# Folding the input through all head matrices first, in four column strips, and weighing all heads into one bank

## The chip, the cores and the metric

The kernel runs on one core of a Trainium2 chip. The metric is the device time of one execution in microseconds (us), from the first to the last instruction. Three runs of the kernel before gave 2040.4, 2041.68 and 2044.19 us; the median is 2041.68 us. The core's engines run side by side and meet through semaphores: PE (TensorE, matrix products, results in the eight PSUM banks), PEld (its weight loads), DVE (VectorE), ACT (ScalarE), POOL (GpSimd) and SP (the queue that starts DMAs). Each engine works off its own instructions in the order in which they are written.

## The reference, cut to what matters

The input is x, 2 x 1024 tokens of 128 features. It is normalised, and the output is x plus two branches of the normalised input: one latent attention layer over the full causal length, and a stack of six layers of windowed attention and gated feed-forward. The change touches the stack:

```python
for i in range(DEPTH):                       # 6 layers
    x = attn_layer(shift_tokens(x), Wqkv[i], q_scale[i], k_scale[i], Wo[i]) + x
    x = ffn_layer(shift_tokens(x), ln_g[i], ln_b[i], W1[i], b1[i], W2[i], b2[i]) + x

def attn_layer(x, Wqkv, qs, ksc, Wo):        # 16 heads of 64, window 32
    q, k, v = split_heads(x @ Wqkv)
    q = rotary(l2norm(q) * qs) ; k = rotary(l2norm(k) * ksc)
    attn = softmax(8 * q @ k_own_and_previous_block, masked)
    return concat_heads(attn @ v) @ Wo

def ffn_layer(x, g, bln, W1, b1, W2, b2):
    a, gate = split((layernorm(x) * g + bln) @ W1 + b1)   # 2 x 341
    return a * gelu(gate) @ W2 + b2
```

shift_tokens takes the upper 64 features from the token before. For one head the output is P (x Wv) Wo, where P is 32 queries by 64 keys for each block of 32 tokens. Both kernels form the folded matrices M_h = Wv_h Wo_h, 128 x 128, once a layer (16 heads), and so need no values or head outputs of their own.

## The kernel before, in words

The stack works on 96 tiles of 128 tokens (16 tiles a layer, 6 layers), in a software pipeline. Each engine has one list of stages, written out by hand in a loop `for G in range(STEPS)`; in step G a stage works on tile G, G-1, G-2 and so on, whatever its argument says. Nothing but these lists and the waits on semaphores sets the order of the work.

For a tile PE projects keys and queries (`project`, float32r in three products of an upper and a lower part, six matmuls of 512 columns each), transposes keys and queries by head pairs (`transposes`, eight of 128x128), writes a mask into banks 4 and 5 and adds the scores onto it (`mask_scores`, `scores`, 64 small matmuls), transposes the softmax's result (`transpose_probs`), and then applies it. Banks 0 and 1 hold a projection, 2 and 3 transposes, 4 and 5 the scores, 6 and 7 everything small and the feed-forward. A stage that writes a bank first claims it: `claim` waits until the last reader of the bank is done (the dictionary `freed`).

The application of the probabilities is what the change replaces. Before, `input_rows` transposes the shifted input back into rows (L1324), ACT copies it (L710), SP copies it by ten DMAs a tile into windows of 64 rows (L351 to L354, doubled on two halves of the partitions), `weigh` multiplies rows of the input by the probabilities, 64 keys deep (two halves of four matmuls of 256 columns, banks 4 and 5), ACT copies the result (L717, L723), and `fold` multiplies it by the sixteen M_h (16 matmuls of 128x128 with 128 columns, bank 7). The sum lies with features on the partitions. DVE adds it to X (`attended`, L981); two transposes and a copy bring rows for the layer norm (`ln_rows`, L1399).

On DVE a step has for keys and for queries a cosine product (L934), a sine product (L939) and a sum of squares (L961, L966), then denominators, moments, maxima and subtraction of the softmax, and `seeds` (L992, L994, L997, L1000), four small operations on 33 columns, which begin a reciprocal square root. ACT goes on with it in `roots` (a logarithm and an exponential, L764, L766) and POOL ends it in `refine` (L501). POOL also adds cosine and sine products (L471, L476), scales keys, queries and probabilities (L507, L513, L466). Every four tiles make a chunk of 512 tokens for the feed-forward: `up_gate`, `up_value` (3 matmuls each, three slices j = 0, 1, 2 of 341), the gelus on ACT (L774) and `down`. The gelu needs another table of functions on ACT than logarithm and exponential; after gelu j = 2 the line `act.preload_act_table_set("natural_log_exp_and_others")` (L777) fetches the latter, and the compiler puts a load in front of any other activation whose function the table in force lacks.

## Time and profile before

| quantity | value |
|---|---|
| median of 3 runs | 2041.68 us (2040.4 to 2044.19) |
| the profiled execution, its own time | 2045.28 us |
| its span, first to last instruction | 2043.4 us |
| busy: PE, DVE, ACT, POOL | 1873.4, 1656.8, 1264.6, 1331.1 us |
| granted PE clock, mean | 0.982 |
| ACT table loads in the program | 50 |

The span has three stretches. To about 365 us the latent attention runs, which the change leaves as it is but for where a few arrays lie. From 368.6 to 1966.4 us the 96 tiles enter the pipeline one after the other, and the rest is the pipeline running empty. Busy time is time in which at least one instruction of an engine runs; PE's matmuls overlap, so that the length of a piece of PE's work is best read from the start of it to the start of the next.

### The profile page before, as it was taken

The page shows a single profiled execution, that of the slowest core. Times are in us where ns is not written, and L with a number is a line of the kernel's source. Part 1 is how long each engine was busy: PE and PEld are TensorE (multiplying, and loading weights), DVE is VectorE, ACT ScalarE, POOL GpSimd, SP SyncE. Part 2 cuts the span into 40 slices and gives each one's busy share as a digit, 9 for nine tenths or more (in the row PEclk, how much of TensorE's full clock was granted, in tenths as well). Part 3 has the DMA queues.
Part 4 walks back from the last instruction along what each step waited for, and adds up shares of the span by engine and source line. Part 5 has one row for each costly group of instructions (what it writes and reads, how often), then busy time and mean ns, then how long its engine had stood idle before and what let it go on. Part 6 is the DMA issues. An engine that isn't in the chain of part 4 may idle for free.

```text
span 2043.4 us, 61163 instructions
## 1 busy us (share of the span) xinstructions
PE 1873.4 (92%) x24364; PEld 1471.0 (72%) x24364; DVE 1656.8 (81%) x2684; ACT 1264.6 (62%) x2082; POOL 1331.1 (65%) x1146
## 2 busy tenths in 40 slices
PE   6888887598999999999999999999999999999996
PEld 4655656477777777777777777777777777777774
DVE  4866866577888898898879998898989889887873
ACT  5766665355666566656655666566666666665653
POOL 3322334477778776787767886777777778776760
PEclk9999998799999999999999999999999999999999
DMA  3000000011001110010111101100111001000001
GB/s 106 2 0 0 0 1 6 22 38 38 22 18 24 39 40 17 22 25 18 39 38 22 24 19 39 37 22 22 25 39 38 20 21 24 18 18 15 19 18 27
DMA packets 76933, 50.06 MB, mean 24 GB/s; under 512 B 17216, under 2 KB 74240, under 8 KB 75008
## 3 DMA queue, kind: packets, MB, share of 16 engines
q1 hardware_dynamic: 76672, 46.39, 9.0%
q8 instruction: 187, 3.06, 0.6%
q14 instruction: 74, 0.61, 0.1%
HBM read 20.11 MB, written 1.05 MB: 10 GB/s over the span
## 4 chain that ended last, share of the span: by engine, by line
PE 62%; DVE 23%; issue 9%; ACT 4%; POOL 1%; DMA 1%; DVEq 0%; SPq 0%; ACTq 0%; POOLq 0%
PE banks L1101 44%; PE banks L1258 9%; DVE arena L939 4%; PE banks L1310 4%; DVE arena L934 3%; DVE small L885 2%; PE banks L1185 2%; DVE small L1005 2%; DVE small L966 2%; PE banks L1299 1%; DVE lnx L1020 1%; DVE small L961 1%; DVE arena L1048 1%; DVE small L997 1%; DVE small L972 1%
## 5 line engine op out<-in xcount | busy, mean ns | idle before, releaser
L1101 PE MATMUL banks<-arena 128*128 128x128 f32 (+3 forms) x4516 | 450.9, 280 | 32.3 <-DMA arena<-in_wqT_dram 10.1
L1101 PEld LDWEIGHTS banks<-arena 128*128 128x128 f32 (+3 forms) x4516 | 426.5, 173 | 69.8 <-issue 19.1
L471 POOL TENSOR_TENSOR arena<-arena 128x1024 f32<-128x1024 f32 x96 | 228.8, 2383 | 110.0 <-DVE arena L939 110.0
L934 DVE TENSOR_TENSOR arena<-banks,tabs 128x1024 f32<-128x1024 f32 x192 | 234.3, 1220 | 62.4 <-PE banks L1258 52.7
L703 ACT ACTIVATE arena<-banks 128x1024 f32<-128x1024 f32 x96 | 98.6, 1027 | 230.9 <-PE banks L1258 230.9
L939 DVE TENSOR_TENSOR arena<-banks,tabs 128x1024 f32<-128x1024 f32 x192 | 232.9, 1213 | 0.2 <-issue 0.2
L466 POOL TENSOR_TENSOR prob<-prob,small 128x1024 f32<-128x1024 f32 x96 | 182.8, 1904 | 74.2 <-DVE small L974 70.3
L476 POOL TENSOR_TENSOR arena<-arena 128x1024 f32<-128x1024 f32 x96 | 228.5, 2380 | 0.0
L1101 PE MATMUL banks<-arena,xwr 64*128 64x256 f32 x1536 | 217.8, 402 | 11.3 <-ACT arena L717 11.3
L1101 PE MATMUL banks<-qkH,xsH 128*128 128x512 f32 x384 | 173.7, 452 | 39.6 <-DVE arena L939 39.6
L1258 PE MATMUL banks<-cst,arena 128*128 128x128 f32 x1536 | 209.5, 280 | 0.1
L513 POOL TENSOR_TENSOR arena<-arena,small 128x1024 f32<-128x1024 f32 x96 | 185.1, 1928 | 14.0 <-POOL arena L476 0.4
L1258 PEld LDWEIGHTS banks<-cst,arena 128*128 128x128 f32 x1536 | 176.7, 143 | 21.0 <-issue 1.7
L1101 PEld LDWEIGHTS banks<-arena,xwr 64*128 64x128 f32 x1536 | 132.2, 186 | 81.7 <-issue 47.8
L501 POOL TENSOR_TENSOR small<-small 128x33 f32<-128x33 f32 x100 | 24.7, 247 | 248.3 <-ACT small L766 248.3
L507 POOL TENSOR_TENSOR arena<-arena,small 128x1024 f32<-128x1024 f32 x96 | 182.8, 1904 | 4.4
L966 DVE TENSOR_REDUCE small<-arena 128x16 f32<-128x1024 f32 x96 | 116.8, 1216 | 83.3 <-ACT arena L679 82.9
L394 POOL TENSOR_TENSOR gqs<-arena,cst 128x128 fp32r<-128x128 f32 x112 | 46.0, 411 | 186.9 <-PE banks L1101 157.2
L668 ACT ACTIVATE arena<-banks 128x1024 f32<-128x1024 f32 x96 | 98.5, 1026 | 95.5 <-PE banks L1101 95.5
L1101 PE MATMUL banks<-qkH,xsL 128*128 128x512 f32 x384 | 155.1, 404 | 0.0
L1101 PE MATMUL banks<-qkL,xsH 128*128 128x512 f32 x384 | 154.2, 402 | 0.0
L1310 PE MATMUL banks<-arena 64*32 64x64 f32 x12288 | 143.8, 226 | 10.4 <-issue 9.1
(135 smaller groups left out, 4217.6 us busy)
## 6 DMA issues: line engine op xcount, KB each, us to landing
xwr<-xwr SPq DMA_DIRECT2D x576, 32.0 KB, 1.9
qkraw<-in_wqk_dram SPq DMA_DIRECT2D x6, 1024.0 KB, 5.2
arena<-in_wvo_dram SPq DMA_DIRECT2D x6, 1024.0 KB, 5.2
xwr<-xwr SPq DMA_DIRECT2D x384, 16.0 KB, 1.8
W<-in_w_dram SPq DMA_DIRECT2D x6, 341.0 KB, 3.1
W<-in_w_dram SPq DMA_DIRECT2D x6, 192.0 KB, 2.7
res<-in_x_dram SPq DMA_DIRECT2D x4, 256.0 KB, 4.2
tabc<-in_tab_dram SPq DMA_DIRECT2D x1, 1024.0 KB, 7.5
```

The lines of the kernel that those rows point to most:

```text
L466: pool.tensor_tensor(p, p, over(den[:, :], 64), ALU.mult).then_inc(s["p_nrm"], 1)
L471: pool.tensor_tensor(kc, kc, ks, ALU.add).then_inc(s["k_add"], 1)
L476: pool.tensor_tensor(qc, qc, qs, ALU.add).then_inc(s["q_add"], 1)
L507: pool.tensor_tensor(heads(kc), heads(kc), over(rs[:, 4, 0:LH], LD), ALU.mult).then_inc(s["k_nrm"], 1)
L513: pool.tensor_tensor(heads(qc), heads(qc), over(rs[:, 4, LH:2 * LH], LD), ALU.mult).then_inc(s["q_nrm"], 1)
L703: act.activation(ptile[:, :, :], two(2).rearrange("p (k t) -> p k t", k=NP), ACT.Copy).then_inc(s["pt_cp"], 1)
L934: dve.tensor_tensor(heads(c), heads(two(0)), table(k % NT, kind), ALU.mult).then_inc(s[done], 1)
L939: dve.tensor_tensor(w.rearrange("p (h z k) -> p h z k", h=LH, z=2), swapped(two(0)), table2(k % NT, kind + 1), ALU.mult).then_inc(s[done], 1)
L966: dve.reduce_sum(rin[:, LH:2 * LH], heads(sqq), AXX).then_inc(s["q_ss"], 1)
L1101: return pe.matmul(o, l, r, start=start, stop=stop)
L1258: ins = pe.transpose(bk(2 + k // 4)[:, P * (k % 4):P * (k % 4 + 1)], src[:, P * k:P * (k + 1)], ident)
L1310: ins = pe.matmul(bk(4 + o)[WIN * w:WIN * (w + 1), 64 * j:64 * (j + 1)], qT[r, j, WIN * w:WIN * (w + 1)], kT[r, j, WIN * w:WIN * w + 64], ...
```

## The change

Products are taken in the other order. The shifted input, 32 tokens at a time (stationary, 128x32), is multiplied by all sixteen M_h at once: `values`, two groups a tile, eight matmuls of 512 columns each, four of them side by side in the four 32-column strips of the array, each with another quarter of M as its moving operand. ACT copies each group of 64 tokens (two banks, 1024 columns) into a ring of six (`vw`). Then `weigh` multiplies by the transposed probabilities, 128 keys-by-heads deep, again in four strips (one for each block of 32 queries), 32 matmuls of 128 columns into one bank, which is the weighed sum of all heads, with tokens on the partitions. Gone are `input_rows`, the row copy, the ten DMAs a tile, `fold` and the two copies between `weigh` and `fold`. The probabilities lie otherwise for this (own half and previous half apart), so that the access patterns of `subtract`, `denominators` and `scale_probs` change, not their sizes.

Since the sum now has tokens on the partitions, the residual stream (`Xt`) is kept so too. `ln_rows` becomes a product with a shifted unit matrix, a second one of 32 rows takes the token before the tile, and ACT copies 64 columns twice. `down` swaps its operands (12 matmuls of 128 columns for 3 of 512, the same number of columns, b2 as a row of W2). Once a chunk PE transposes the new stream into columns (`layer_columns`, four transposes) and ACT copies it (`copy_layer`).

`seeds` moves from DVE to POOL, right in front of `refine`. `normalise_rows` is a scalar_tensor_tensor in place of a tensor_scalar. And the lists of stages of all engines are written in a new order with other lags; STEPS grows from 107 to 108. On SP the loads of the next layer's weights no longer stand behind the row DMAs and their waits. `lower_shifted` on POOL is one operation of 128x512 for two of 64x512 and a memset. The diff, cut:

```diff
-STEPS = DEPTH * TILES + 11
+STEPS = DEPTH * TILES + 12
-M_BANK, XT_BANK, DN_BANK = 7, 6, 7
+PV_BANK, V_BANK, XT_BANK, DN_BANK, LN_BANK = 6, 4, 7, 7, 7
...
+            def values(k, g):
+                b, i = tile_at(k)
+                pe.wait_ge(s["xs"], 2 * (k // 4) + 2)
+                pe.wait_ge(s["M_H"], 2 * (k // TILES) + 2)
+                claim(V_BANK, V_BANK + 1)
+                for z in range(2):
+                    t0 = P * i + 64 * g + WIN * z
+                    for q in range(NQ):
+                        ins = pe.matmul(bk(V_BANK + z)[WIN * q:WIN * (q + 1), :], xs[:, b, t0:t0 + WIN],
+                                        M[:, q, :, :].rearrange("p m n -> p (m n)"), start=True, stop=True, skip_group_check=True)
...
+            def weigh(k):
...
+                    for z in range(2):
+                        for m in range(NQ):
+                            for w in range(NW):
+                                ins = pe.matmul(bk(PV_BANK)[WIN * w:WIN * (w + 1), 0:D], ptile[:, NQ * z + m, WIN * w:WIN * (w + 1)],
+                                                block_of(k, w - 1 + z)[:, D * m:D * (m + 1)],
+                                                start=(z, m) == (0, 0), stop=(z, m) == (1, NQ - 1), skip_group_check=True)
...
+            def copy_values(k, g):
+                act.wait_ge(s[f"v_mm{g}"], k + 1)
+                after(act, "o_mm", k - 2 + g)
+                act.activation(vw[:, (2 * k + g) % RV, :], two(V_BANK), ACT.Copy).then_inc(s[f"v_cp{g}"], 1)
...
# DVE: normalise_rows
-                    dve.tensor_scalar(lnx[:, :], lns[:, k % 2, :], ag[:, k % 2, 0:1], rs[:, 4, 32:33], ALU.subtract, ALU.mult)\
+                    dve.scalar_tensor_tensor(lnx[:, :], lns[:, k % 2, :], ag[:, k % 2, 0:1],
+                                             rs[:, 4, 32:33].to_broadcast([P, D]), ALU.subtract, ALU.mult).then_inc(s["ln_x"], 1)
...
# POOL, list of stages (new)
+                next_table(G - 2)
+                lower_columns(G - 7)
+                rotate_keys(G - 1)
+                scale_probs(G - 3)
+                shifted_lower(chunk_at(G, 15))
+                seeds(G - 1)
+                refine(G - 1)
+                scale_keys(G - 1)
+                next_query_weights(G - 1)
+                rotate_queries(G - 1)
                 lookback(G - 1)
...
# ACT, list of stages (new)
+                copy_columns(G - 6)
+                copy_values_upper(G - 2)
+                roots(G - 1)
+                gelu(chunk_at(G, 10), 0)
+                copy_layer(chunk_at(G, 14))
...
+                copy_probs(G - 3)
+                gelu(chunk_at(G, 11), 1)
...
+                gelu(chunk_at(G, 10), 2)
                 square_keys(G)
+                shifted_upper(chunk_at(G, 14))
+                copy_rows(G - 4)
+                exponentials(G - 2)
+                copy_keys(G - 1)
+                copy_values_lower(G - 1)
                 square_queries(G)
# DVE, list of stages (new)
+                maxima(G - 2)
                 normalise_rows(G - 5)
+                gated(chunk_at(G, 11), 0)
+                subtract(G - 2)
                 cosine_keys(G)
                 sine_keys(G)
+                attended(G - 3)
+                denominators(G - 2)
+                moments(G - 4)
                 sum_keys(G)
+                sum_queries(G)
+                cosine_queries(G)
+                gated(chunk_at(G, 11), 1)
+                sine_queries(G)
+                gated(chunk_at(G, 11), 2)
+                residual(chunk_at(G, 12))
```

PE's list shows best in the built programs. Before, in the step in which the gate slice j = 2 (85 columns wide) is computed, PE has behind the transposes of the queries:

```order
L1101 MATMUL banks<-xnH,W1H 85x512
L1101 MATMUL banks<-xnH,W1L 85x512
L1101 MATMUL banks<-xnL,W1H 85x512
L1101 MATMUL banks<-arena 128x128 x8
L1407 MATMUL banks<-cst,lnx 128x128
L1299 MATMUL banks<-bfc 128x512 x2
L1101 MATMUL banks<-arena 128x128 x8
L1310 MATMUL banks<-arena 32x64 x64
L1258 MATMUL banks<-cst,prob 128x128 x8
```

The other two gate slices stand earlier in that same step, behind the transposes of the keys, and the scores are followed by the transposes of the probabilities. Now, in the step that computes the gate slices 0 and 2 (L1311 is `values`, L1438 `layer_columns`, L1286 the mask, L1245 the transposes, L1297 the scores):

```order
L1311 MATMUL banks<-M,xs 32x512 x8
L1089 MATMUL banks<-xnw,w1w 128x512 x3
L1438 MATMUL banks<-cst,Xt 128x128 x4
L1286 MATMUL banks<-bfc 128x512 x2
L1245 MATMUL banks<-cst,prob 128x128 x8
L1297 MATMUL banks<-arena 32x64 x64
L1089 MATMUL banks<-xnw,w1w 85x512 x3
```

Gate slice 2, which uses bank 6 as slice 0 does, now stands right behind the scores and in front of the projection of the keys (six rows at L1089 that follow).

On ACT, the step with the gelus before (L774 gelu, L764 and L766 `roots`, L679 and L697 copies for the queries):

```order
L774 ACT_TABLE_LOAD
L774 ACTIVATE arena<-banks,b1p 128x512
L723 ACTIVATE arena<-banks 128x2x512
L774 ACTIVATE arena<-banks,b1p 128x512
L679 ACTIVATE arena<-banks 128x1024
L774 ACTIVATE arena<-banks,b1p 85x512
L777 ACT_TABLE_LOAD
L697 ACTIVATE arena<-banks 128x1024
L756 ACTIVATE xnf<-banks 128x128
L757 ACTIVATE xnH<-banks 128x128
L764 ACTIVATE small<-small 128x33
L766 ACTIVATE small<-small 128x33
```

All three gelus share one load in front and one behind, and `roots` has none. The same place now (L719 `copy_values_upper`, L773 and L775 `roots`, L783 gelu, L592 and L593 `copy_layer`, L714 `copy_probs`, L786 the preload, L679 the squares of the keys):

```order
L719 ACTIVATE arena<-banks 128x1024
L773 ACT_TABLE_LOAD
L773 ACTIVATE small<-small 128x33
L775 ACT_TABLE_LOAD
L775 ACTIVATE small<-small 128x33
L783 ACT_TABLE_LOAD
L783 ACTIVATE arena<-banks,b1p 128x512
L592 ACTIVATE xs<-banks 64x512
L593 ACTIVATE xs<-banks 64x512
L714 ACTIVATE arena<-banks 128x1024
L783 ACTIVATE arena<-banks,b1p 85x512
L786 ACT_TABLE_LOAD
```

The gelu of slice 1 has moved to the step after the preload; `roots` has a load in front of the logarithm and another in front of the exponential. The whole program has 230 table loads where it had 50: 67 each at L773 and L775, 48 at L783, 24 at L786, 22 in front of the softmax's exponential (L745), 2 at the start.

## Rows read from the trace of the kernel before

**Rows 1.** The page: busy time, share of the span and instructions by engine.
```profile
PE 1873.4 (92%) x24364; PEld 1471.0 (72%) x24364; DVE 1656.8 (81%) x2684; ACT 1264.6 (62%) x2082; POOL 1331.1 (65%) x1146
```

**Rows 2.** Stretches: length, busy PE, PEld, DVE, ACT, POOL (instructions), clock, DMA share, GB/s.
```profile
700.00:1900.00 1200.00, 1158.45 (x16133) 918.01 (x16131) 1050.41 (x1425) 765.95 (x1136) 893.91 (x660) 1.00 0.11 27
...
1966.00:2043.40 77.40, 59.74 (x605) 42.81 (x603) 37.98 (x75) 35.23 (x59) 21.07 (x21) 0.98 0.10 25
```

**Rows 3.** The squares of the keys: ns min/median/max, first and last start.
```profile
L668 ACT ACTIVATE arena<-banks x96: 1024/1026/1032, 368.6 to 1966.4; 128x1024 f32<-128x1024 f32 x96
```

**Rows 4.** Waits from 700 to 1900 us: total, times, longest us.
```profile
POOL small L501 <- ACT small L766: 169.7, 71, 4.9
...
PE banks L1101 <- DVE arena L939: 20.7, 30, 0.9
```

**Rows 5.** PE in order of time, one step: start, us, instruction, shapes, count.
```profile
1203.53 0.28 PE L1324 MATMUL banks<-cst,X 64*128 64x64 f32 x2
1203.74 1.09 PE L1258 MATMUL banks<-cst,arena 128*128 128x128 f32 x8
...
1207.41 1.13 PE L1101 MATMUL banks<-arena,xwr 64*128 64x256 f32 x8
1208.48 0.50 PE L1101 MATMUL banks<-qkH,xsH 128*128 128x512 f32 x1
...
1209.97 1.03 PE L1258 MATMUL banks<-cst,arena 128*128 128x128 f32 x8
1210.84 1.95 PE L1101 MATMUL banks<-arena 128*128 128x128 f32 x16
1212.63 0.27 PE L1407 MATMUL banks<-cst,lnx 128*128 128x128 f32 x1
1212.73 0.59 PE L1299 MATMUL banks<-bfc 128*128 128x512 bf16 x2
1213.17 1.95 PE L1101 MATMUL banks<-arena 128*128 128x128 f32 x16
1215.04 1.48 PE L1310 MATMUL banks<-arena 64*32 64x64 f32 x128
1216.46 1.09 PE L1258 MATMUL banks<-cst,prob 128*128 128x128 f32 x8
```

**Rows 6.** PE in the latent attention, matmuls in four 32-column strips, and what follows.
```profile
310.75 1.74 PE L1101 MATMUL banks<-arena 128*32 128x128 f32 x56
312.42 0.44 PE L1185 MATMUL banks<-cst,arena 128*128 128x128 f32 x2
```

**Rows 7.** ACT in order of time: the softmax's exponential, a table load, a gelu.
```profile
1258.09 1.05 ACT L741 ACTIVATE prob<-prob 128x1024 f32<-128x1024 f32 x1
1259.15 1.28 ACT L774 ACT_TABLE_LOAD   x1
1260.44 0.69 ACT L774 ACTIVATE arena<-banks,b1p 128x512 f32<-128x512 f32 x1
```

**Rows 8.** In order of time: `seeds`' last operation, `roots` on ACT, `refine` on POOL.
```profile
1215.14 1.25 DVE L1000 TENSOR_TENSOR small<-small 128x33 f32<-128x33 f32 x1
...
1216.42 0.23 ACT L764 ACTIVATE small<-small 128x33 f32<-128x33 f32 x1 [3.04 <-DVE small L1000]
...
1216.69 0.23 ACT L766 ACTIVATE small<-small 128x33 f32<-128x33 f32 x1
1217.06 0.25 POOL L501 TENSOR_TENSOR small<-small 128x33 f32<-128x33 f32 x1 [0.71 <-ACT small L766]
```

**Rows 9.** Groups from 700 to 1900 us: busy us, mean ns, idle before.
```profile
L513 POOL TENSOR_TENSOR arena<-arena,small 128x1024 f32<-128x1024 f32 x70 | 135.5, 1936 | 10.0
...
L412 POOL TENSOR_TENSOR xsL<-X,xsH 64x512 fp32r<-64x512 f32 x18 | 23.4, 1300 | 1.4
...
L939 DVE TENSOR_TENSOR arena<-banks,tabs 128x1024 f32<-128x1024 f32 x141 | 170.9, 1212 | 0.0
L1020 DVE TENSOR_SCALAR lnx<-lns,small 128x128 f32<-128x128 f32 x70 | 91.4, 1306 | 0.0
```

More of the change, by code:

```diff
@@ L22 @@
 AXX = mybir.AxisListType.X
+AXXY = mybir.AxisListType.XY
 P = 128
@@ L244, in chunk_at, with columns @@
             return c if (G - lag) % 4 == 0 and 0 <= c < DEPTH * NC else None
+        def columns(c):
+            b, t0 = divmod(c % NC * CH, T)
+            return X[:, b, t0:t0 + CH]
         def layer_at(G, lag):
@@ L746, in copy_rows, with copy_layer @@
                     after(act, "ln_x", k - 1)
-                    act.activation(lns[:, k % 2, :].rearrange("p (z c) -> p z c", z=2),
-                                   two(6).rearrange("p (z c) -> p z c", z=2)[:, :, 0:64], ACT.Copy).then_inc(s["ln_cp"], 1)
+                    act.activation(lns[:, k % 2, 64:D], bk(LN_BANK)[:, 0:64], ACT.Copy).then_inc(s["ln_cp"], 1)
+                    act.activation(lns[:, k % 2, 0:64], Xt[:, k % TILES, 0:64], ACT.Copy).then_inc(s["ln_cp"], 1)
+            def copy_layer(c):
+                if c is not None and c < (DEPTH - 1) * NC:
+                    act.wait_ge(s["xT_mm"], c + 1)
+                    shifted(c + NC, bk(XT_BANK))
             def copy_columns(k):
@@ L1313, in scores @@
                     ins.then_inc(s["s_mm"], 1)
-            def input_rows(k):
-                if is_tile(k):
-                    b, i = tile_at(k)
-                    after(pe, "x_new", k // 4 - NC + 1)
-                    claim(XT_BANK, XT_BANK + 1)
-                    for z in range(2):
-                        r = slice(64 * z, 64 * z + 64)
-                        c0 = XO + P * i - z
-                        ins = pe.transpose(bk(XT_BANK + z)[:, XT_COL:XT_COL + 64], X[r, b, c0:c0 + P], ident[r, 64 * z:64 * z + 64])
-                    ins.then_inc(s["xT_mm"], 1)
-                    freed[XT_BANK] = freed[XT_BANK + 1] = ("xT_cp", k + 1)
@@ L1328, in weigh @@
-            def weigh(k, half):
-                claim(4, 5)
-                for w2 in range(2):
-                    w = 2 * half + w2
-                    for o in range(2):
-                        r = slice(64 * o, 64 * o + 64)
-                        ins = mm(bk(4 + o)[:, 256 * w2:256 * (w2 + 1)].rearrange("p (k t) -> p k t", k=NP),
-                                 xw[r, k % 2, w, :], ptile[r, :, WIN * w:WIN * (w + 1)])
-                ins.then_inc(s["z_mm"], 1)
-                freed[4] = freed[5] = ("z_cp", 2 * k + half + 1)
@@ L1341, in weigh_lower, with values_lower, values_upper @@
+            def values_lower(k):
+                if is_tile(k):
+                    values(k, 0)
+            def values_upper(k):
+                if is_tile(k):
+                    values(k, 1)
+            def weigh(k):
                 if is_tile(k):
                     pe.wait_ge(s["pt_cp"], k + 1)
[L1343 to L1356 removed]
+                    pe.wait_ge(s["v_cp0"], k + 1)
+                    pe.wait_ge(s["v_cp1"], k + 1)
+                    pe.wait_ge(s["vw_0"], 1)
+                    claim(PV_BANK)
+                    for z in range(2):
[4 more added lines that the diff above has]
+                                                start=(z, m) == (0, 0), stop=(z, m) == (1, NQ - 1), skip_group_check=True)
+                    ins.then_inc(s["o_mm"], 1)
+                    freed[PV_BANK] = ("x1", k + 1)
@@ L1392, in ln_rows @@
                 if is_tile(k):
-                    b, i = tile_at(k)
+                    n = k % TILES
                     pe.wait_ge(s["x1"], k + 1)
-                    claim(6, 7)
-                    for z in range(2):
-                        r = slice(64 * z, 64 * z + 64)
-                        c0 = 1 + P * i - z
-                        ins = pe.transpose(bk(6 + z)[:, 0:64], X1[r, b, c0:c0 + P], ident[r, 64 * z:64 * z + 64])
+                    claim(LN_BANK)
+                    ins = mm(bk(LN_BANK)[:, 0:64], next_row, Xt[:, n, 64:D])
+                    if n % NT:
+                        ins = pe.matmul(bk(LN_BANK)[0:32, 0:64], first_row, Xt[96:P, n - 1, 64:D], start=False, stop=True,
+                                        skip_group_check=True)
                     ins.then_inc(s["lnT_mm"], 1)
-                    freed[6] = freed[7] = ("ln_cp", k + 1)
+                    freed[LN_BANK] = ("ln_cp", 2 * k + 2)
             def ln_columns(k):
```

402 lines of the change are left out of this document (157 added, 245 removed).

## The prediction

> **What bounds the kernel now.** I began with busy time by engine: PE is busy for 92% of the span [rows 1]. The table of stretches then says where: from 700 to 1900 us PE is busy for 1158.45 of 1200 us at a full clock, DVE for 1050, POOL for 894, ACT for 766 [rows 2]. The squares of the keys mark one step a tile; 95 steps lie between 368.6 and 1966.4 us, so a step takes 16.82 us [rows 3], and 1200 us hold 71.3 of them. Per step PE is busy 16.24 us and idle 0.58, DVE busy 14.7, POOL 12.5, ACT 10.7. The list of waits shows what idles PE: the sine product on DVE for 20.7 us in 30 waits, so 0.29 us a step [rows 4]. POOL has slack, and shows it as a wait of 2.4 us a step for ACT's roots, 169.7 us in all [rows 4]. So PE's own work sets the pace, with DVE 2 us behind it. A change is worth what it takes from PE's step, if no loop through ACT, DVE and POOL becomes longer than PE's step.
>
> **PE's work.** I read lengths from start to start [rows 5]. Removed per tile: input rows 1203.53 to 1203.74, 0.2 us; two halves of weighing at 1207.41 to 1208.48, 2 x 1.07 = 2.14; two halves of folding, 1.79 + 1.87 = 3.66. Sum 6.0 us. Added: the trace has the new shape in the latent attention. There 8 key blocks in 4 strips make 64 records of 128 columns (each float32 matmul leaves two; 56 of the 64 are in the trace), and they take 310.75 to 312.42 = 1.67 us [rows 6]. `weigh` now is 64 such records, 1.67 us; a group of `values` is 16 records of 512 columns, as many columns, again 1.67 us. Three times that is 5.0; for leaving and entering the strips I add 0.3, so 5.3 us. The row product for the layer norm has full weights and a second part of 32 rows: +0.2. `layer_columns` is four transposes a chunk, 4 x 0.11 over 4 steps: +0.1. `down` keeps its columns; its 24 records at 1.79/16 = 0.11 us give 2.7 us a chunk, as now. PE's unstalled step is 16.24 - 6.0 + 5.3 + 0.3 = 15.85 us. The unknown in it is a strip matmul of 512 columns. From below, 1.67 us a group is already four strips at once. From above, the scores are the nearest row that packs less well: 128 records of 64 columns in eight tiles take 1.42 us [rows 5], so 1024 columns per tile, against 2048 per tile in 1.67 us; at the scores' pace the three groups would take 3 x 2.84 = 8.5 us. I take 1.67, whose shape is the same.
>
> Here a page speaks against the change. The Trainium skill, "TensorE: Matmul & The Clock Gate", Part 3, on measured speedup, gives four packed tiles 3.07 times and three column strips 2.38 times the rate of one, not four and three. By that rule 5.0 us become 5.0 x 4 / 3.07 = 6.5, 1.5 us more a step. The 1.67 us of rows 6 disagree with it.
>
> **DVE.** It loses the four seeds, of which the last alone took 1.25 us for 33 columns in rows 8, while POOL's 0.25 us for as many columns is the least that one can cost. So at least 1 us a step goes. `normalise_rows` takes 1.31 us on average for 128 columns [rows 9], of which the columns explain little. The new form costs between 0.25 us, the price of a small operation, and 1.3 as now; I take 1.0, near its own row. DVE falls below 13.7 us a step, no bound by sum.
>
> **POOL.** It loses one of two operations of 1.3 us a chunk (-0.35 us a step [rows 9]) and gains four seeds. The nearest price of a small operation there is `refine`, 0.25 us [rows 8]; with a handoff between dependent ones 4 x 0.32 = 1.3. So 13.5 us busy, 13.8 with gaps. But `seeds` and `refine` now stand next to each other, and POOL sits idle while ACT does the roots. At best that is what the trace shows, 1216.39 (end of the seed) to 1217.06 = 0.67 us [rows 8].
>
> **ACT, and the term that decides.** Copies come out even (two of 1.03 us for two). But the built program has 230 table loads for 50, 10 in 4 steps where there were 2. A load takes 1.28 us, and the gelu follows 0.01 us behind its end [rows 7]. That is +2.6 us a step, ACT at 13.6 us: again no bound by sum, but ACT's list is in order and other engines wait in it. The Trainium skill, "ScalarE: Activation LUTs", What ACT_TABLE_LOAD costs, adds a drain of about 1.38 us to the 1.283 us of a load. Rows 7 show none: exponential ends 1259.14, load starts 1259.15. With a drain the chain of three loads below would be 3 x 1.38 = 4.1 us longer in one step of four.
>
> Let t be the end of the second group of `values` on PE. ACT copies it: t+1.15. In three steps of four a load for the logarithm (to t+2.45), the logarithm, a load (to t+4.0) and the exponential follow: roots end at t+4.2. In the step of gate slices 0 and 2 comes a third load and the gelu of slice 0: t+5.5, t+6.25. PE meanwhile does gate slice 0 (0.75), layer_columns (0.45), mask (0.44), transposes (0.87 and a switch, 1.05) and scores (1.42) [rows 5], so that at t+4.15 it stands before gate slice 2, whose bank 6 is freed by that gelu. First loss: 6.35 - 4.15 = **2.2 us**. ACT goes on: two column copies (to 7.5), probabilities (8.5), gelu 2 (9.2), the preload (10.5), and only then the squares of the keys (11.55). DVE's cosine and sine products (2 x 1.21) follow to t+14.0, and PE's next projection, the queries, needs their end: 14.1. PE itself would be there at 6.35 + 0.7 (gate) + 1.5 (keys) + 0.95 (transposes) + 0.5 (rows) + 1.75 + 1.75 (weigh, values) = 13.5. Second loss: **0.6 us**.
>
> In the step with up-value slices 1 and 2 the path is POOL's. From the start P of the queries' projection, t = P+4.3. DVE needs after sine_keys 0.3 + 1.4 + 0.6 + 1.15 + 1.15 us to the sum of the queries, so seeds end at P+5.9 = t+1.6, before the logarithm's load is over. Roots end t+4.2, refine t+4.6, scaled keys +1.94 [rows 9] = t+6.6. PE wants them for its transposes at t + 1.5 + 0.44 + 1.05 + 1.42 + 1.5 = t+5.9. Loss **0.7 us**. In the step with `down` that is covered by its 2.7 us. In the step without loads in `roots`, gated slice 0 (0.74 us) stands in front of the subtraction on DVE: from the scores' end maxima 1.35, normalise 1.0, gated 0.74, subtract 1.15, cosine 1.15, sine 1.21 and handoffs 0.3 are 6.9 us, against PE's 6.4 (keys 1.5, transposes 0.9, rows 0.5, weigh 1.75, values 1.75). Loss **0.5 us**.
>
> Together 2.2 + 0.6 + 0.7 + 0.5 = 4.0 us in 4 steps, 1.0 a step. The step is 15.85 + 1.0 = 16.85, and for the loops that pass within 0.3 us of PE's (POOL's ring in a step with loads is 13.8 + 2.9 = 16.7) I add 0.05: **16.9 us**.
>
> **Edges.** Four more column copies on ACT as the latent attention starts, 4 x 0.6 = 2.4 us at most. The pipeline runs empty in 77.4 us over 11 steps [rows 2]; a twelfth is added and the last transposes go. I take +5 us for both, between 0 and 12. The row DMAs go, ten a tile; they cost nothing now, since no DMA is among the waits of PE in rows 4's stretch, and the weights' loads on SP, which stood behind them, can only come earlier. The latent stretch, 365 us, stays.
>
> **Sum.** 95 x (16.90 - 16.82) = +8, +5: 13 us more than the profiled execution's 2045.28, so 2058. That execution stood 3.6 us above the median, against which the forecast is 2041.7 + 13 = 2055, say **2054 us**. What PE saves (0.4 us a step of work and most of 0.58 us idle) goes back into table loads.
>
> **Rivals.**
> A. The loads are hidden better. For it: ACT is busy 13.6 of 16.9 us, and if seeds come late the logarithm's load is over before them; against it: the gelu chain has three loads in a row whatever seeds do. If only 1.8 us in four steps are lost, the step is 16.3, and the time 2041.7 - 49 + 5 = **1997 us**; with nothing lost 15.95 a step, 1964.
> B. POOL's ring becomes the bound. It decides from where the round trip over ACT is longer than 16.9 - 13.8 = 3.1 us, that is, when seeds end more than 0.2 us after ACT was ready and both loads lie open behind each other's waits, or when the small operations cost 0.5 us each in place of 0.3. At 17.5 us a step: 2041.7 + 65 + 5 = **2111 us**, slower. For it: rotation, three scalings and seeds leave POOL no room; against it: one step in four has no loads and lets it catch up.
> C. Four strips don't run at four times the pace. Rows 6 speak against it, though only for 128 columns. At 2.2 us a group, between rows 6 and the scores' pace, it is +1.6 us a step and **2204 us**. By the 3.07 of the Trainium skill's "TensorE: Matmul & The Clock Gate" it would be 1.5 x 95 more than the forecast, 2197 us.
> D. A load holds ACT for longer than its row when another load or an exponential comes right behind. Rows 7 show 0.01 us behind a load; if the chain were 4 us longer in one step of four, it would be +95 us, **2149 us**. It is the drain of the Trainium skill's "ScalarE: Activation LUTs".
>
> **How the numbers follow.** Forecast 0.47, A 0.32, B 0.16, C 0.03, D 0.02. A difference of 0.2%, 4 us, is about what a measurement of this kernel can tell. The forecast's own range is 2030 to 2080: of its 0.47, 0.07 is faster than 2037.6, 0.10 is within 0.2%, 0.30 slower. A is faster for 0.30 and the same for 0.02; B, C and D are slower. Faster 0.37, same 0.12, slower 0.51. The range runs from inside A (below 1985 I leave 0.08) to B's middle (above 2112, 0.11).
>
> **What would show it.** In the profile after: `weigh` and each `values` group near 1.7 us from start to start (right: PE's work per step 15.8 to 16); table loads busy about 295 us in all; in one step of four an idle PE in front of gate slice 2, released by a gelu; POOL's `refine` waiting for ACT 2 to 3 us a step; the transposes of the keys waiting for POOL. Wrong: no gap before gate slice 2 (then A), POOL above 90% busy or waiting nowhere else than for the roots (B), strips above 2 us a group (C).

## The result, and the profile after

The changed kernel takes **2081.29 us** (median of 4 runs, 2079.05 to 2089.52), the kernel before beside it 2041.04 us (4 runs, 2037.65 to 2044.19). The ratio is 1.0205, 95% interval 1.0172 to 1.0238: slower by 40 us. The forecast was 2054 us, slower by 13; the measured time lies 1 us above the forecast's own range (2030 to 2080) and well inside the outer one (1985 to 2112).

The profiled execution spans 2080.7 us. Its busy row, to be held against [rows 1]:

```profile
PE 1849.6 (89%) x29444; PEld 1308.2 (63%) x29444; DVE 1529.7 (74%) x2286; ACT 1501.6 (72%) x2286; POOL 1399.4 (67%) x1494
```

PE works 24 us less than before, and ACT 237 us more. Next the stretch of [rows 2] (length, then busy PE, PEld, DVE, ACT, POOL, clock, DMA share, GB/s), and the squares of the keys, which mark a step as in [rows 3]:

```profile
700.00:1900.00 1200.00, 1110.02 (x19216) 775.74 (x19219) 925.57 (x1110) 922.17 (x1253) 916.68 (x879) 0.99 0.03 10
```
```profile
L679 ACT ACTIVATE arena<-banks x96: 1005/1025/1032, 363.5 to 1996.0; 128x1024 f32<-128x1024 f32 x96
```

A step is (1996.0 - 363.5) / 95 = 17.18 us, where it was 16.82. Of the 37 us between the two spans the 95 steps make 1632.5 - 1597.8 = 35, the start is 5 us earlier and the drain (1996.0 to 2080.7 us, before 1966.4 to 2043.4) some 8 us longer. The 1200 us hold 69.8 steps. In each of them PE is busy for 15.90 us, where it was 16.24, and idle for 1.29, where it was 0.58. So PE's work did shrink, and its idle time grew by twice as much. The waits in that stretch say what ended the idle time (engine, tile and line, released by; total us, times, longest):

```profile
POOL small L506 <- ACT small L775: 154.2, 68, 3.3
...
DVE arena L943 <- ACT arena L679: 64.1, 21, 3.6
...
PE banks L1089 <- ACT arena L783: 38.6, 17, 2.3
...
PE banks L1297 <- issue: 16.3, 24, 1.0
...
PE banks L1089 <- DVE arena L948: 10.4, 33, 0.3
PE banks L1335 <- DVE arena L1039: 10.2, 15, 1.3
...
PE banks L1245 <- ACT M L731: 8.2, 4, 2.2
...
PE banks L1311 <- DVE prob L1001: 2.3, 5, 0.6
...
PE banks L1245 <- POOL arena L512: 0.6, 1, 0.6
```

Read the rows that begin with PE. The largest is the wait of gate slice 2 (L1089) for a gelu (L783), 17 times 2.3 us, once in four steps; in [rows 4] the largest was the sine product, 20.7 us in 30 waits. The sine product (L948) is now 10.4. New are the scores' "issue" (L1297: nothing that the profile shows was waited for), the weighing's wait (L1335) for the gated product (L1039), and, at a change of layer, the transposes (L1245) behind ACT's copy of the next folded matrices (L731).

The table loads on ACT, by the line of the operation that they stand in front of (count in the stretch, busy us, mean ns, idle before):

```profile
L773 ACT ACT_TABLE_LOAD x51 | 65.4, 1283 | 0.9
L775 ACT ACT_TABLE_LOAD x51 | 65.4, 1283 | 0.9
L783 ACT ACT_TABLE_LOAD x34 | 43.6, 1283 | 0.6
...
```

L773 and L775 are logarithm and exponential of `roots`, L783 the gelus. The preload (L786) and the softmax's exponential (L745) have 17 more each: 170 loads, 218 us. Here is one step of the gate, cut to the rows that follow one another (start, us, engine and line, in brackets the idle time before and its releaser):

```profile
1199.17 1.92 PE L1311 MATMUL banks<-M,xs 128*32 128x512 f32 x16
...
1201.02 0.96 PE L1089 MATMUL banks<-xnw,w1w 128*128 128x512 f32 x3
...
1201.16 1.03 ACT L719 ACTIVATE arena<-banks 128x1024 f32<-128x1024 f32 x1 [0.52 <-PE banks L1311]
...
1202.21 1.28 ACT L773 ACT_TABLE_LOAD   x1
...
1203.66 1.49 PE L1297 MATMUL banks<-arena 64*32 64x64 f32 x128
1203.75 1.28 ACT L775 ACT_TABLE_LOAD   x1
1205.05 0.23 ACT L775 ACTIVATE small<-small 128x33 f32<-128x33 f32 x1
...
1205.29 1.28 ACT L783 ACT_TABLE_LOAD   x1
...
1206.59 0.69 ACT L783 ACTIVATE arena<-banks,b1p 128x512 f32<-128x512 f32 x1
...
1207.42 0.90 PE L1089 MATMUL banks<-xnw,w1w 128*85 128x512 f32 x3 [2.27 <-ACT arena L783]
...
1210.01 1.28 ACT L786 ACT_TABLE_LOAD   x1
...
1211.30 1.02 ACT L679 ACTIVATE arena<-banks 128x1024 f32<-128x1024 f32 x1
...
1212.42 1.23 DVE L943 TENSOR_TENSOR arena<-banks,tabs 128x1024 f32<-128x1024 f32 x1 [3.56 <-ACT arena L679]
...
1214.92 0.47 PE L1089 MATMUL banks<-qkH,xsH 128*128 128x512 f32 x1 [0.29 <-DVE arena L948]
```

The values' second group starts at 1199.17 and PE goes on at 1201.02, the prediction's t. ACT copies it, loads for the logarithm, loads for the exponential, loads for the gelu, and the gelu of slice 0 ends at 1207.28, t+6.26, where t+6.25 was worked out. PE had finished the scores and stood idle for 2.27 us. Then gelu 2 and the preload hold up the squares of the keys (L679); DVE waits 3.56 us for them, and its sine product releases the queries' projection at 1214.92, 0.29 us late.

### The profile page after: what moved, and what is told of

Its sections match the earlier page's. It is cut to its first block and busy times, and to the rows that moved or that the text cites. A ratio compares the mean times of both kernels' runs of the same rounds, so it can differ in the third digit from the quotient of the medians.

```text
span 2080.7 us, 70693 instructions
## 1 busy us (share of the span) xinstructions
PE 1849.6 (89%) x29444; PEld 1308.2 (63%) x29444; DVE 1529.7 (74%) x2286; ACT 1501.6 (72%) x2286; POOL 1399.4 (67%) x1494
## 5 line engine op out<-in xcount | busy, mean ns | idle before, releaser
L1311 PE MATMUL banks<-M,xs 128*32 128x512 f32 x3072 | 369.0, 596 | 3.8 <-DVE prob L1001 3.6
L995 DVE TENSOR_REDUCE small<-banks 128x16 f32<-128x1024 f32 x96 | 117.5, 1224 | 211.2 <-PE banks L1297 211.2
L719 ACT ACTIVATE arena<-banks 128x1024 f32<-128x1024 f32 x192 | 197.2, 1027 | 100.2 <-PE banks L1311 97.3
L948 DVE TENSOR_TENSOR arena<-banks,tabs 128x1024 f32<-128x1024 f32 x192 | 232.7, 1212 | 0.0
L1245 PE MATMUL banks<-cst,arena 128*128 128x128 f32 x1536 | 204.9, 277 | 2.4 <-POOL arena L512 1.7
L1335 PE MATMUL banks<-arena 128*32 128x128 f32 x6144 | 190.4, 276 | 11.0 <-DVE arena L1039 10.6
L1245 PEld LDWEIGHTS banks<-cst,arena 128*128 128x128 f32 x1536 | 179.2, 142 | 29.2 <-issue 5.0
L1089 PE MATMUL banks<-qkH,xsH 128*128 128x512 f32 x384 | 172.5, 449 | 23.6 <-DVE arena L948 21.8
L1089 PE MATMUL banks<-xnw,w1w 128*128 128x512 f32 (+1 forms) x432 | 130.1, 430 | 57.0 <-ACT arena L783 55.8
L1335 PEld LDWEIGHTS banks<-arena 128*32 128x32 f32 x6144 | 164.7, 111 | 20.9 <-issue 14.2
L1311 PEld LDWEIGHTS banks<-M,xs 128*32 128x32 f32 x3072 | 90.2, 109 | 137.4 <-issue 135.0
L679 ACT ACTIVATE arena<-banks 128x1024 f32<-128x1024 f32 x96 | 98.3, 1024 | 105.8 <-PE banks L1089 105.5
L1297 PE MATMUL banks<-arena 64*32 64x64 f32 x12288 | 150.7, 227 | 22.5 <-issue 22.5
L1297 PEld LDWEIGHTS banks<-arena 64*32 64x32 f32 x12288 | 130.0, 106 | 44.0 <-issue 44.0
```

Of the source, the lines that this page charges most:

```text
L719: act.activation(vw[:, (2 * k + g) % RV, :], two(V_BANK), ACT.Copy).then_inc(s[f"v_cp{g}"], 1)
L948: dve.tensor_tensor(w.rearrange("p (h z k) -> p h z k", h=LH, z=2), swapped(two(0)), table2(k % NT, kind + 1), ALU.mult).then_inc(s[done], 1)
L1089: return pe.matmul(o, l, r, start=start, stop=stop)
L1245: ins = pe.transpose(bk(2 + k // 4)[:, P * (k % 4):P * (k % 4 + 1)], src[:, P * k:P * (k + 1)], ident)
L1297: ins = pe.matmul(bk(4 + o)[WIN * w:WIN * (w + 1), 64 * j:64 * (j + 1)], qT[r, j, WIN * w:WIN * (w + 1)], kT[r, j, WIN * w:WIN * w + 64], ...
L1311: ins = pe.matmul(bk(V_BANK + z)[WIN * q:WIN * (q + 1), :], xs[:, b, t0:t0 + WIN], M[:, q, :, :].rearrange("p m n -> p (m n)"), start=True ...
```

## The experiments

All times are medians, and ratios are to the kernel before, run beside them (2046.76 us in the first set: e1 to e4; 2045.48 in the second: e5, e6, e7, e9; 2048.4 in the third: e10, e11).

**e1, no loads in `roots`.** One more preload, behind gelu 1; the built program has 98 table loads, not 230.

```diff
-                    if j == LAST_GELU:
+                    if j in (1, LAST_GELU):
                         act.preload_act_table_set("natural_log_exp_and_others")
```

> The changed kernel with one more preload of the set that holds logarithm and exponential, behind the gelu of slice 1: 98 table loads in the program for 230, none left in roots. Theory L (the loads are what ate the saving): the wait before gate slice 2 (2.27 us in each of 24 steps, 55.8 us in the whole trace) goes, POOL's wait for the roots falls from 2.3 to about 0.7 us a step, and the step falls from 17.18 us to 16.1-16.4: 1985 to 2010 us. Rival P (PE's own work in strips, with the gaps in the scores, is what made it slower, and the loads lie beside it): not more than 15 us come back, 2065 to 2081 us.

Measured: 2002.84 us, ratio 0.9795 (0.9754 to 0.9837). A step is 16.35 us. Its stretch and three of its waits:

```profile
700.00:1900.00 1200.00, 1157.04 (x20371) 813.24 (x20370) 960.96 (x1167) 837.45 (x1216) 966.94 (x928) 1.00 0.03 10
```
```profile
POOL small L506 <- ACT small L775: 44.1, 73, 0.6
...
PE banks L1297 <- issue: 21.7, 26, 1.2
PE banks L1335 <- DVE arena L1039: 11.3, 14, 1.3
...
PE banks L1089 <- ACT arena L783: 0.2, 1, 0.2
```

The wait before gate slice 2 falls from 38.6 to 0.2 us, POOL's for the roots from 154.2 to 44.1, and the wait for the folded matrices is gone from the list. One line in ACT's program turns the change from 2% slower into 2% faster. That is the loads' price where they stand: 78 us by the medians, 84 by the ratios, 0.83 us a step by the trace. Of the 0.83, PE's idle time makes 0.70 (1.29 to 0.59 a step) and its busy time 0.13 (15.90 to 15.77), although PE's work is the same; the section on the prediction comes back to this.

**e4, the loads put into the kernel before.** The converse: without the preload the compiler places 91 + 91 + 26 = 208 loads there, for 50.

```diff
-                    if j == LAST_GELU:
-                        act.preload_act_table_set("natural_log_exp_and_others")
```

> The kernel before without its preload behind the gelus: the compiler then puts 91 loads each before logarithm and exponential of roots, 208 loads for 50. Theory L: the round trip over ACT grows by 1.3 to 2.6 us in three of four steps. POOL waited 2.4 us a step there, but scaled keys are needed at once by PE, and DVE's list goes on behind: 40 to 110 us slower, 2080 to 2150 us. Rival P: ACT is busy 10.7 of 16.8 us in that kernel, the loads fall into its idle time: within 15 us of 2041.

Measured: 2049.94 us, ratio 1.0021 (0.9996 to 1.0047): no difference that can be told. The loads are there, ACT's busy time in the stretch rises from 765.95 [rows 2] to 924.48 us, and POOL's wait for the roots from 169.7 [rows 4] to 266.0:

```profile
700.00:1900.00 1200.00, 1158.20 (x16131) 915.91 (x16129) 1025.01 (x1419) 924.48 (x1261) 891.04 (x660) 1.00 0.11 26
```
```profile
POOL small L501 <- ACT small L766: 266.0, 71, 7.6
```

PE is busy for 1158.20 us of it, as before. The expectation that loads cost by their number fell. In the order of before the one who waits behind them is POOL, and it has the slack for it.

**e10, fewer loads in one place only.** In the step in front of a gate step the logarithm's set is fetched early, behind the softmax's exponential.

```diff
                 exponentials(G - 2)
+                if chunk_at(G + 1, 10) is not None:
+                    act.preload_act_table_set("natural_log_exp_and_others")
```

> The changed kernel with the set of logarithm and exponential fetched once a chunk right behind the softmax's exponential of the step before gate slices 0 and 2, so that roots has no loads in that step and in the two around it that had none or lose them, while one step in four (with up-value slices 1 and 2) keeps both: 162 loads for 230. Theory L (the chain of three loads in front of the gelu of slice 0 carries most of the loss, as the predicted 2.8 of 4.0 us in four steps): the wait before gate slice 2 goes, and of the 78 us that the second preload won at least two thirds come, 2005 to 2030 us. Rival E (the loads cost by their number, spread over all steps): of 132 loads that the second preload saved 68 go, so half of 78 us, 2035 to 2050 us.

Measured: 2025.58 us, ratio 0.9894 (0.9857 to 0.9932). The expectation miscounted the loads: the built program has 210, since two steps of four keep both loads of `roots`. So it is even clearer than was planned: 20 loads fewer than the changed kernel's 230, and 3.1% or 63 us come back by the ratios, where e1 took 132 away for 4.1% or 84. The wait before gate slice 2 (here L1091) is down to nothing:

```profile
PE banks L1091 <- ACT arena L783: 0.5, 2, 0.3
```

e1, e4 and e10 together show that a load costs by the chain that it stands in.

**e2, the gelu ahead of `roots`.** The gate no longer waits behind the two other loads; the program has 254.

```diff
-                roots(G - 1)
                 gelu(chunk_at(G, 10), 0)
+                roots(G - 1)
```

> The changed kernel with the gelu of slice 0 written ahead of roots on ACT, loads left as the compiler puts them (254 for 230). Theory L: the wait before gate slice 2 goes (2.27 us in one of four steps, 54 us in all), but roots end later (behind a gelu and its load, 2 us) so that POOL's scaled keys come later in that step, and the squares of the keys stay late: 10 to 30 us faster than the changed kernel, 2050 to 2070 us. Rival P: the wait is PE's slack in another place, within 5 us of 2081.

Measured: 2113.9 us, ratio 1.0339 (1.0295 to 1.0383), so 1.3% slower than the changed kernel, against the expectation. The wait of the gate for the gelu is gone, and in its place stands this:

```profile
PE banks L1245 <- POOL arena L512: 38.7, 18, 2.3
```

The roots come later, POOL scales the keys later, and PE's transposes of the keys (L1245) wait the same 2.3 us. The chain of three loads has two customers, and the order only chooses which of them is late. That alone would be an even exchange, 38.7 us for 38.6. The step is 17.54 us for 17.18 because PE also idles 0.16 us more a step in smaller waits and because its busy time, for the same work, grows by 0.19: its clock is lower more often (see below).

**e7, the waiting instruction moved.** Gate slice 2 goes behind the transposes of the keys on PE.

```diff
-                up_gate(chunk_at(G, 10), 2)
                 next_shifts(chunk_at(G, 12))
                 project_keys(G)
                 transpose_keys(G - 1)
+                up_gate(chunk_at(G, 10), 2)
```

> The changed kernel with gate slice 2 behind the transposes of the keys in PE's list, loads as they are. It takes away the wait of 2.27 us in front of gate slice 2, but not ACT's chain: the copy of the probabilities, on which those transposes wait, and the squares of the keys stay behind the loads, and gelu 2 comes later. Theory L (ACT's chain, not the bank): the wait turns up again in front of the transposes of the keys and the queries' projection, within 15 us of 2081. Rival W (the wait before gate slice 2 is the loss itself): 30 to 54 us faster, 2027 to 2050 us.

Measured: 2145.28 us, ratio 1.0498 (1.0463 to 1.0534), 2.9% or some 60 us slower than the changed kernel. Both expectations were wrong. Waits, and a piece of ACT in order of time:

```profile
DVE arena L943 <- ACT arena L679: 108.2, 20, 7.2
...
PE banks L1245 <- ACT arena L714: 48.0, 17, 2.8
ACT arena L783 <- PE banks L1089: 46.2, 16, 3.5
```
```profile
1245.49 0.68 ACT L783 ACTIVATE arena<-banks,b1p 85x512 f32<-85x512 f32 x1 [3.43 <-PE banks L1089]
...
1247.49 1.02 ACT L679 ACTIVATE arena<-banks 128x1024 f32<-128x1024 f32 x1
```

PE reaches the gate without waiting, but later; now gelu 2 waits 3.43 us for it on ACT, and the preload and the squares of the keys behind it come later still. DVE's wait for them grows from 64.1 to 108.2 us. I had moved the waiter and lengthened the chain. A step is 17.86 us, 0.68 more: 0.45 of it is idle time of PE and 0.22 busy time for the same work, at a lower clock.

**e3, the old form of `normalise_rows`.** Only the form goes back; the two read the same numbers.

```diff
-                    dve.scalar_tensor_tensor(lnx[:, :], lns[:, k % 2, :], ag[:, k % 2, 0:1],
-                                             rs[:, 4, 32:33].to_broadcast([P, D]), ALU.subtract, ALU.mult).then_inc(s["ln_x"], 1)
+                    dve.tensor_scalar(lnx[:, :], lns[:, k % 2, :], ag[:, k % 2, 0:1], rs[:, 4, 32:33], ALU.subtract, ALU.mult)\
+                       .then_inc(s["ln_x"], 1)
```

> The changed kernel with the tensor_scalar of the kernel before in normalise_rows. The new form takes 1546 ns on average for 128 columns where the old took 1306. Theory L: DVE waits for PE's scores 2.1 us a step, so the form costs nothing but in steps where the subtraction is late: within 5 us of 2081. Rival N (the new form waits more for POOL and delays subtraction and sine products): the mean falls back to 1.3 us and the time by 10 to 20 us.

Measured: 2084.39 us, ratio 1.0185 (1.0143 to 1.0228), the changed kernel's within the intervals. The group in the changed kernel (700 to 1900 us), and in e3 (whole span):

```profile
L1010 DVE SCALAR_TENSOR_TENSOR lnx<-lns,small 128x128 f32<-128x128 f32 x69 | 106.7, 1546 | 0.0
```
```profile
L1010 DVE TENSOR_SCALAR lnx<-lns,small 128x128 f32<-128x128 f32 x96 | 146.7, 1528 | 8.2 <-POOL small L506 8.2
```

1546 and 1528 ns: the form changes nothing. I had put the new form at 1.0 us.

**e5 and e6, `seeds` back on DVE,** behind the sum of the queries; e5 from the changed kernel, e6 from e1. The four operations are the same.

```diff
                 shifted_lower(chunk_at(G, 15))
-                seeds(G - 1)
                 refine(G - 1)
...
                 sum_queries(G)
+                seeds(G)
                 cosine_queries(G)
```

> The changed kernel with seeds back on DVE, behind sum_queries, loads as they are. Theory L (ACT's chain of loads and gelu sets the step; POOL's list only matters through it): seeds end at about the same time on either engine, so within 8 us of 2081. Rival R (with seeds in front of refine, POOL's own ring of 13.8 us and the round trip is what the loads lengthen): POOL gets 1.1 us a step back, 20 to 50 us faster, 2030 to 2060 us.

> The kernel with the second preload (2003 us) and seeds on DVE as well. POOL waits there 1.8 us a step for the sine product, DVE 2.1 us for the scores, so neither is bound by its sum. Theory: within 6 us of 2003, so that the move of seeds to POOL earns nothing here. Rival R: POOL's relief shows, 10 to 20 us faster. Rival D (the seeds' small operations wait on DVE for POOL, as 1.25 us did for one of them in the kernel before, and make the sine product of the queries late): 8 to 25 us slower.

Measured: e5 2072.16 us, ratio 1.0148 (1.0114 to 1.0183); e6 1986.49 us, ratio 0.9724 (0.9691 to 0.9756), the fastest kernel here. e6 lies 16 us under e1 and e5 some 12 (0.6% by the ratios) under the changed kernel; the intervals of e6 and e1 just touch, and those of e5 and the changed kernel overlap by little. e6's step is 16.23 us for e1's 16.35. Its stretch and waits:

```profile
700.00:1900.00 1200.00, 1167.96 (x20506) 821.04 (x20505) 1044.46 (x1473) 842.78 (x1230) 900.74 (x644) 1.00 0.03 10
```
```profile
DVE small L994 <- PE banks L1297: 73.9, 65, 2.0
PE banks L1297 <- issue: 18.1, 24, 1.2
...
PE banks L1335 <- DVE arena L1038: 4.5, 7, 0.7
```

DVE works 84 us more than in e1 and yet less waits for it: the weighing's wait for the gated product falls from 11.3 to 4.5 us, and PE is busy for 97.3% of the stretch. DVE stood idle anyway, 153.3 us for the scores in e1 and now 73.9.

**e9, one strip of four.** From e1; three quarters of the folded matrices are left out of the attention, so that a group of `values` has 4 records of 512 columns and not 16.

```diff
-                    for q in range(NQ):
+                    for q in range(1):
```

> The kernel with the second preload, in which values computes the first of the four strips alone and copies 32 partitions of it (three quarters of the folded matrices are left out of the attention; the ring is zeroed once). Theory S (the four strips run side by side): a group keeps the length of one strip's columns, 4 records of 512 columns at about 0.43 us = 1.7 us of the 1.9 now, and the time falls by at most 2 x 0.25 us a step, 1980 to 2003 us. Rival C (the strips share the columns' rate in part, as a packing of 3.07 would have it): a group falls to 1.3 us or less and the time to 1900 to 1960 us.

Measured: 1988.89 us, ratio 0.9733 (0.9702 to 0.9764). A group and what follows it on PE, in e9 and then in e1:

```profile
1209.07 1.88 PE L1312 MATMUL banks<-M,xs 128*32 128x512 f32 x4
1210.88 0.50 PE L1090 MATMUL banks<-qkH,xsH 128*128 128x512 f32 x1
```
```profile
1213.35 1.92 PE L1311 MATMUL banks<-M,xs 128*32 128x512 f32 x16
1215.20 0.49 PE L1089 MATMUL banks<-W,arena 128*128 128x128 f32 x2
```

From start to start 1.81 us with one strip and 1.85 with four: the other three ride along for 0.04 us. e9 is 0.6% faster than e1 all the same, though the two intervals overlap a little; PE's part of that is 2 x 0.04 x 95 = 8 us. The smaller copies on ACT and the scores' gaps (10.6 us in 14 for 21.7 in 26) may make the rest, which I did not separate.

**e11, the scores ahead of the transposes of the probabilities,** from e6.

```diff
-                transpose_probs(G - 3)
                 scores(G - 2)
+                transpose_probs(G - 3)
```

> The kernel with the second preload and seeds on DVE (1986 us), with PE's scores in front of the transposes of the probabilities. PE's work is the same. DVE waits there 1.0 us a step for the scores and would get them 0.9 us earlier, which PE can only use if it waits for DVE; it waits 0.1 us a step for it. Theory (PE's own work is the bound, busy 97.3%): 1978 to 1990 us. Rival (the loop from the maxima to the projection of the queries still sets the step): 10 to 20 us faster, 1966 to 1978 us; and if copies of the transposed queries are late for the scores, slower by up to 20 us.

Measured: 2007.51 us, ratio 0.9803 (0.9765 to 0.9842), slower than e6 by 16 us by the ratios and 21 by the medians. PE idles for 52.6 us of the stretch, where it was 32.0. The largest of its waits is new:

```profile
PE banks L1089 <- ACT arena L764: 14.7, 18, 0.9
```

L764 is the gelu in this kernel. In the trace the one that waits, 18 times and mostly 0.93 us, is the first product of `ln_rows`: it uses bank 7, which the gelu of slice 1 reads. The wait of the queries' projection for the sine product grows from 5.8 to 13.6 us beside it. There was nothing left to win by this exchange.

## Why the prediction was right in sign and short in size

The mechanism was the one that the prediction named: PE saves work and gives it back to table loads that stand in the ordered list of ACT. The forecast was a step of 16.90 us; it is 17.18. Of this come 0.28 x 95 = 27 us; the edges cost 3 us for the 5 forecast, and so the profiled spans stand 37 us apart and not 13 (the medians 40). By the prediction's own steps:

**PE's work, 15.85 us a step: 15.90 measured,** and 15.77 in e1. Inside it, a group of strips was put at 1.67 us with 0.3 for all switches; start to start it is 1.85 us (1199.17 to 1201.02). So the added strips cost some 0.25 us more than worked out, and something else at least as much less than worked out; which part, no row here settles.

**PE's clock: a term that the sum did not have.** The prediction worked at a full clock. Behind some of its waits PE works on for a while at a granted clock of 0.50, which is 1.2 GHz in place of 2.4. Here is one wait before gate slice 2; the first row is a stretch of 1 us, whose granted clock of 0.50 stands third from its end:

```profile
715.00:716.00 1.00, 0.84 (x2) 0.62 (x3) 1.00 (x2) 0.97 (x3) 1.00 (x2) 0.50 0.00 0
```
```profile
715.16 1.55 PE L1089 MATMUL banks<-xnw,w1w 128*85 128x512 f32 x3 [2.28 <-ACT arena L783]
716.50 0.63 PE L1089 MATMUL banks<-qkH,xsH 128*128 128x512 f32 x1
```

The same two rows at the full clock take 0.90 and 0.40 us (1207.42 and 1208.16). From 700 to 1900 us the clock falls so 9 times in the changed kernel: 4 times behind a wait for the gelu (of 17 such waits), twice behind the folded matrices' copy and 3 times behind a gap in the scores; the kernel before and e1 have 3 falls each. Why only some of the waits are followed by one is not shown. Taken over slices of 1 us, what the clock lacks of 1.00 adds up to 15.4 us here, 5.1 before, 5.1 in e1, 25.6 in e2 and 33.9 in e7. As an estimate, this is the time lost while PE is busy: 0.22 us a step for 0.07 before, so 0.15 of the 0.36 by which the step grew, or some 14 of the 40 us. Two things agree with it: PE's busy time falls by 0.13 us a step in e1, whose work is the same, and the mean clock was 0.970 to 0.976 in all four runs of the changed kernel, 0.980 to 0.982 in those of e1. At the clock of before, PE's step would have been some 15.75 us, so that 15.90 for 15.85 is partly luck: the work was put 0.1 too high, and the clock made up for it.

**First loss, 2.2 us in four steps: 38.6 us over 17.45 sets of four = 2.2.** It was read off ACT's list as a chain, copy, load, load, load, gelu, with the lengths of rows of before, and every link came true to a few hundredths.

**Second loss, 0.6: 10.4 / 17.45 = 0.6,** though in 33 short waits, of which the gate step has one of 0.29. e1 keeps 6.7 of the 10.4 us, so only a third of it hangs on the loads. That the number came true is luck for the most part.

**Third loss, 0.7 for late scaled keys: 0.07** (L1245 for POOL, 1.2 us in 4 waits). PE, itself later than in my sum, found them ready. In e2, where the roots were put behind the gelu, this wait appeared with 38.7 us: the path is there, with some slack that I had not counted.

**Fourth loss, 0.5 for DVE's loop with a gated product: 0.7,** mostly at another instruction. The wait of `values` for the subtraction (L1311) is 2.3 us, and the weighing's for the gated product itself (L1335) 10.2; 12.5 / 17.45 = 0.7. e1 keeps it and e6 halves it, so it is DVE's and POOL's order and not the loads. Here too the size is nearer than the place.

Together 3.6 us in four steps for 4.0. **The step that failed is the one behind the four losses,** "I add 0.05". What PE waited for beyond them was: gaps in which nothing was waited for, 16.3 + 2.2 = 18.5 us or 0.27 a step, where the kernel before has 9.3 us in 1200, 0.13 a step; and the folded matrices' copy at a change of layer, 8.2 us or 0.12 a step. The latter is a fifth customer of ACT's chain of loads, gone in e1. With these and PE's 15.90, slower clock included, the step is 15.90 + 0.89 + 0.27 + 0.12 = 17.18 us. A quiet mistake stands behind the first: I let all of the 0.58 us of idle time of the kernel before disappear because its causes were moved, though 0.13 of it were gaps without a releaser, for which the new order took away no known cause.

**The price of the loads** as a term was near: what hung on them was (2.2 + 0.6 + 0.7) / 4 = 0.88 us a step, and e1 shows 0.83. Its parts were others: of PE's waits e1 removes 38.4 us before the gate, 8.2 for the folded matrices, 3.7 for the sine product, 2.3 and 1.2 for subtraction and scaled keys, 54 us or 0.77 a step. Longer gaps in the scores take some of that back, to 0.70, and the clock adds 0.13. Without them the change would have come to 2002.84 us, a gain of 2%, and not to the 1964 that rival A gave for nothing lost: 16.35 us a step and not 15.95, of which 0.32 are the gaps.

**`seeds` at no cost to anyone** was wrong by about 15 us (e5, e6). The sum had only POOL's busy time, where they fit. On DVE they run in time that is idle anyway, while on POOL, as I read it, they hold up `refine` and the scalings behind it; the waits of e6 show the gain at the gated product, not the whole way to it.

**Rivals.** A is what one more preload makes of the kernel (e1, 2002.84 us for its 1997), not what it is. B has POOL's wait of 2.2 us a step for the roots for it, as forecast, yet POOL is busy for 916.68 of 1200 us, far from a bound. C falls with e9. The Trainium skill's 3.07 times for four packed tiles ("TensorE: Matmul & The Clock Gate", Part 3, on measured speedup) was measured there on tiles of 32 rows and isn't what these column strips do: 16 records in 1.85 us against 4 in 1.81 is 3.9 times. D falls too: in the gate step the load of 1.28 us at 1203.75 is followed by its exponential at 1205.05, 0.02 us behind, and that one 0.01 us behind its end by the next load. Two figures of the recorded text are off by a slip and change nothing: ACT's 10.7 + 2.6 is 13.3 us a step and not 13.6 (measured 13.2), and C's +1.6 a step on the forecast gives 2206 us and not 2204.

## What to carry to other kernels

Count the table loads in the built program whenever an engine's order changes, and price each by the chain that stands behind it in that engine's list: here 158 more cost nothing that could be told, and 20 fewer gave back about 60 us. If an instruction waits, shorten the chain that ends the wait; moving the instruction or its rival in the list (e2, e7) handed the time to another wait, and the step became longer. Price a wait of PE by more than its length: look at the granted clock behind it, and expect the same work to take longer there. And when a sum of removed work and new losses is done, carry over the idle time of before that no cause explains: it does not go with the rearrangement.

## What the hardware showed that I had not expected

Four column strips of 32, each with its own quarter of the folded matrices moving over the same 32 tokens as weights, cost nearly the same as one: 1.85 and 1.81 us for 1024 float32 columns in each strip (e1, e9).

In the scores PE has gaps with no wait behind them. One in the changed kernel, in order of time:

```profile
1222.22 1.39 PE L1297 MATMUL banks<-arena 64*32 64x64 f32 x116
1224.14 0.33 PE L1297 MATMUL banks<-arena 64*32 64x64 f32 x12 [0.53 <-issue]
```

116 of 128 records run, then 0.53 us pass. There are 24 in 1200 us here for 4 before, and 24 to 26 in e1 and e6, so they came with the change and not with the loads. They belong to places in PE's program and not to moments. The 24 gaps of the changed kernel and the first 24 of e1 stand before the same records: those left of the burst are 14, 19, 7, 7, 31, 19, 24 and so on, in both kernels alike. The count goes with the program too: 14 gaps in e9, where a group of `values` has 12 records fewer, and 9 in e11 with the scores moved, though these are longer (13.0 us in all). The changed kernel's program has 29444 matmul records for 24364 [rows 1]. What sets a gap off was not tried and stays open. At 0.27 to 0.32 us a step it is the largest thing left in e6.

One and the same DVE operation, `normalise_rows` on 128 columns, takes 1306 ns on average before [rows 9], 1546 after, 1329 in e1 and 1249 in e6. Its form has no part in it (e3); what ran beside it on POOL differs between these kernels, but I have no run that isolates that.
